# The expert products of a metaformer block in full fp32 on 64-row tiles, with paired transposes and no split of the second normalization

## The reference

```python
x = x + attention(_ln_c(x))            # over the 16 images at each position, 8 heads of 16 channels, gated
t = x as tokens                        # 65536 rows of 64
t = t + L0_ffn(_ln_t(t))               # 8 experts, the best 2 of each token
x = x + L1_conv(_ln_c(x))              # expand 64 -> 128, running mean along an axis, sigmoid gate, 64 -> 64
t = t + L1_ffn(_ln_t(t))               # 32 experts that each pick 8 tokens of an image
```

```python
def _L0_ffn_ref(x, router_w, router_b, expert_w, expert_b):
    router_probs = jax.nn.softmax(x @ router_w + router_b, axis=-1)
    top_p, top_i = jax.lax.top_k(router_probs, K)                  # K = 2 of 8
    top_p = top_p / jnp.sum(top_p, axis=-1, keepdims=True)
    expert_out = jnp.einsum('bnd,edc->bnec', x, expert_w) + expert_b
    gathered = jnp.take_along_axis(expert_out, top_i[..., None], axis=2)
    return jnp.einsum('bnk,bnkc->bnc', top_p, gathered)
```

## Time and profile before

| what | value |
|---|---|
| three runs | 3127.79, 3136.28 and 3141.26 us |
| median | 3136.28 us |
| span of the profiled execution | 3121.5 us |
| busy PE (matmul) | 2647.5 us, 85% |
| busy PE (weight load) | 1969.9 us, 63% |
| busy DVE | 2551.6 us, 82% |
| busy POOL | 2161.0 us, 69% |
| busy ACT | 2005.1 us, 64% |

### The profile page before, as it was taken

The page is one execution under the profiler, slowest core; times in us unless marked ns, Lnnn a source line. Parts: engine busy times, 40 slices in busy tenths (PEclk is TensorE's granted clock), DMA queues, the critical chain, the costliest instruction groups (busy, mean ns, idle before and its releaser), DMA issues. The chain is left out here.

```text
span 3121.5 us, 108500 instructions
## 1 busy us (share of the span) xinstructions
PE 2647.5 (85%) x37071; PEld 1969.9 (63%) x37071; DVE 2551.6 (82%) x9002; ACT 2005.1 (64%) x3590; POOL 2161.0 (69%) x2963
## 2 busy tenths in 40 slices
PE   2898898888888888898898898888988988896697
PEld 2666666666666656666666666666666666664586
DVE  2788889888888898888888888888889888885604
ACT  2666767766676676776776766677667676762600
POOL 2677777877777777777787877778777777863000
PEclk9788988887888888888887987889889788885858
DMA  0011101111011010110101111011010010101828
GB/s 17 9 20 18 19 17 19 19 18 19 17 19 18 18 19 17 19 19 18 19 17 18 19 18 19 17 19 19 18 19 18 17 19 18 19 15 19 269 96 337
DMA packets 263153, 106.67 MB, mean 34 GB/s; under 512 B 250257, under 2 KB 254900, under 8 KB 258997
## 3 DMA queue, kind: packets, MB, share of 16 engines
q1 hardware_dynamic: 260933, 93.16, 12.9%
q10 hardware_dynamic: 2160, 12.68, 1.0%
HBM read 55.31 MB, written 50.33 MB: 34 GB/s over the span
## 5 line engine op out<-in xcount | busy, mean ns | idle before, releaser
L472 ACT ACTIVATE kT<-s_bank,b_k,block_of 128x512 f32<-128x512 f32 x1024 | 748.8, 771 | 3.6 <-PE s_bank L609 0.3
L640 PE MATMUL s_bank<-kT,qT 128*32 128x128 f32 x8192 | 396.1, 372 | 187.3 <-issue 187.3
L640 PEld LDWEIGHTS s_bank<-kT,qT 128*32 128x32 f32 x8192 | 349.5, 152 | 226.8 <-issue 224.7
L489 ACT ACTIVATE qT<-shared,b_qkg 128x256 f32<-128x256 f32 x256 | 107.5, 471 | 412.0 <-PE shared L609 412.0
L811 DVE TENSOR_REDUCE mixed<-yg 128x256 f32<-128x2048 f32 x128 | 288.5, 2254 | 0.2
L687 PEld LDWEIGHTS o_bank<-w_o,ogT 128*128 128x128 f32 x2048 | 247.9, 193 | 23.7 <-DVE ogT L839 14.8
L414 POOL TENSOR_TENSOR probs<-weights,own_den 128x1024 f32<-128x1024 f32 x128 | 252.7, 1975 | 1.8 <-DVE own_den L857 1.8
L687 PE MATMUL o_bank<-w_o,ogT 128*128 128x64 f32 x2048 | 246.9, 274 | 4.3 <-DVE ogT L839 3.9
L387 POOL TENSOR_TENSOR split_ffn<-norm_ffn,split_ffn 128x256 fp32r<-128x256 f32 x128 | 93.6, 731 | 215.1 <-ACT split_ffn L464 215.1
L658 PEld LDWEIGHTS o_bank<-probsT,v_sb 32*32 32x32 f32 x16384 | 170.2, 107 | 63.7 <-issue 58.1
L658 PE MATMUL o_bank<-probsT,v_sb 32*32 32x64 f32 x16384 | 196.5, 234 | 1.5 <-DVE yg L932 1.5
(11 more groups left out here) (204 smaller groups left out, 7648.6 us busy)
## 6 DMA issues: line engine op xcount, KB each, us to landing
x_in<-in_x SPq DMA_DIRECT2D x1024, 16.0 KB, 1.7
x_scratch<-x SPq DMA_DIRECT2D x1024, 16.0 KB, 1.4
normalized_x_scratch<-norm_pick SPq DMA_DIRECT2D x1024, 16.0 KB, 1.5
xa<-normalized_x_scratch SPq DMA_DIRECT2D x16, 1024.0 KB, 8.1
xb<-x_scratch ACTq DMA_DIRECT2D x8, 1024.0 KB, 10.3
out_x<-xa SPq DMA_DIRECT2D x16, 512.0 KB, 5.3
out_x<-xb SPq DMA_DIRECT2D x16, 512.0 KB, 6.9
xa<-x_scratch SPq DMA_DIRECT2D x4, 1024.0 KB, 6.5
```

Source lines behind the costliest of these rows:

```text
L472: ins = s.activation(kT[:, h, :], bk("k")[:], ACT.Identity, bias=b_k[:, h:h + 1], scale=block_of[:, h:h + 1])
L640: ins = t_.matmul(s_bank[g * 32:(g + 1) * 32, 0, t * P:(t + 1) * P], qT[z][:, c, tok:tok + 32], kT[:, :, tok + c * N:tok + (c + 1) * N], s ...
```

## The change

The expert layer's second operand is no longer split. Four things follow from that.

- **Transposes.** `paired` transposes two token tiles of 64 channels at once: the result has the channels of an even tile on rows 0 to 63 and those of the odd tile after it on rows 64 to 127. Two transposes take the place of four, they wait for the normalization itself, and `tT` is half as wide and in plain fp32.
- **Experts.** A tile is one fp32 product on 64 rows (0 to 63 for y0 and y2, 64 to 127 for y1 and y3) in the place of two one-pass products on 128 rows. As an fp32 product it counts once in the order of instructions below. Weights, the bias rows (`bias3`) and the ones stand in both halves; in the program as built the bias product is on the same 64 rows.
- **Router.** `w_router2` is a block matrix, with the router's weights once for the rows 0 to 63 and once for 64 to 127, so that one product gives the logits of two tiles.
- **Split and order.** The rounding copy of ACT and the subtraction of POOL for `ffn` go. In TURNS, `expand` and `y0` change places, and so in PE's list.

Setup gains a second load of `bias3`, two fills and two small copies, and loses a subtraction and a rounding copy. The diff, cut to its core:

```diff
-TURNS = ["att_t", "q", "ffn_t", "v", "scan_out", "gate", "pick", "conv_t", "y0", "expand", "y3"]
+TURNS = ["att_t", "q", "ffn_t", "v", "scan_out", "gate", "pick", "conv_t", "expand", "y0", "y3"]
...
-            w_expert_hi, w_expert_lo = cb("w_expert_hi", [P, NE * D], F32R), cb("w_expert_lo", [P, NE * D], F32R)
+            w_expert_ce = cb("w_expert_ce", [P, NE * D])
+            w_router2 = cb("w_router2", [P, 2, NE])
...
-            bias3 = cb("bias3", [3, NE * D], BF16)
+            bias3 = cb("bias3", [P, NE * D], BF16)
-            ones3 = cb("ones3", [3, P], BF16)
+            ones3 = cb("ones3", [P, P], BF16)
...
-            KINDS = ("att", "ffn", "conv", "pick")
+            KINDS, SPLIT = ("att", "ffn", "conv", "pick"), ("att", "conv")
-            split = {k: cpair(f"split_{k}", [P, QT, 2, D], F32R) for k in KINDS[:3]}
+            split = {k: cpair(f"split_{k}", [P, QT, 2, D], F32R) for k in SPLIT}
...
-            tT = cpair("tT", [P, QTOK], F32R)
+            tT = cpair("tT", [P, QTOK // 2])
...
-                sp.dma_start(bias3[:], bias_parts[:]).then_inc(s_bias3, 16)
+                for k in range(2):
+                    sp.dma_start(bias3[k * D:k * D + 3], bias_parts[:]).then_inc(s_bias3, 16)
...
                 def step(i, q):
                     if runs(i, q, 4):
                         normalize("ffn", x1[par(q, 4)], 1.0, 1e-5, i, q, 4, "ffn_t")
-                    if runs(i, q, 4):
-                        second_part("ffn", i, q, 4)
...
-                    if runs(i, q, 4):
-                        round_part("ffn", i, q, 4, "ffn_t")
...
                         wait(act, filled["y3"], at(i, q, 6))
-                        s.copy(tT[z][:], bk("ffn_t")[:]).then_inc(drained["ffn_t"], 1)
+                        s.copy(tT[z][:], bk("ffn_t")[:, 0:QTOK // 2]).then_inc(drained["ffn_t"], 1)
...
+                def paired(name, kind, i, q, lag):
+                    for u in range(2):
+                        ins = t_.transpose(bank_of(q, name)[:, u * P:(u + 1) * P],
+                                           norm[kind][par(q, lag)][:, 2 * u:2 * u + 2, :].rearrange("p t d -> p (t d)"), ident[:])
+                    ins.then_inc(filled[name], 1)
...
                             bank_free(pe, i, q, y)
-                        t_.matmul(bk(y)[:], ones3[:], bias3[:], start=True, stop=False)
-                        t_.matmul(bk(y)[:], tT[z4][:, tile(t)], w_expert_hi[:], start=False, stop=False)
-                        t_.matmul(bk(y)[:], tT[z4][:, tile(t)], w_expert_lo[:], start=False, stop=True).then_inc(filled[y], 1)
+                        r0 = t % 2 * D
+                        t_.matmul(bk(y)[:], ones3[r0:r0 + D], bias3[r0:r0 + D], start=True, stop=False)
+                        t_.matmul(bk(y)[:], tT[z4][r0:r0 + D, tile(t // 2)], w_expert_ce[r0:r0 + D], start=False,
+                                  stop=True).then_inc(filled[y], 1)
...
                     if runs(i, q, 4):
                         bank_free(pe, i, q, "ffn_t")
-                        pe.wait_ge(s_split["ffn"], at(i, q, 4))
-                        transposed("ffn_t", "ffn", i, q, 4)
+                        pe.wait_ge(s_norm["ffn"], at(i, q, 4))
+                        paired("ffn_t", "ffn", i, q, 4)
                         bank_free(pe, i, q, "v")
...
                         pe.wait_ge(drained["ffn_t"], at(i, q, 4))
-                        for t in range(QT):
-                            ins = t_.matmul(bk("route")[:, t * NE:(t + 1) * NE], tT[z4][:, tile(t)].bitcast(F32), w_router[:])
+                        for u in range(2):
+                            ins = t_.matmul(bk("route")[:, 2 * u * NE:2 * (u + 1) * NE], tT[z4][:, tile(u)],
+                                            w_router2[:].rearrange("p h e -> p (h e)"))
                         ins.then_inc(filled["route"], 1)
...
                         bank_free(pe, i, q, "conv_t")
                         transposed("conv_t", "conv", i, q, 5)
-                    if runs(i, q, 4):
-                        experts(0)
                     if runs(i, q, 5):
                         bank_free(pe, i, q, "expand")
...
                         t_.matmul(bk("expand")[:], w_expand_hi[:], cT[:], start=True, stop=False)
                         t_.matmul(bk("expand")[:], w_expand_lo[:], cT[:], start=False, stop=True).then_inc(filled["expand"], 1)
                     if runs(i, q, 4):
-                        for t in range(1, QT):
+                        for t in range(QT):
                             experts(t)
...
-                v.tensor_copy(w_expert_hi[:].rearrange("d (c e) -> d c e", e=NE), w_expert[:].rearrange("d e c -> d c e"))
+                setup(v.tensor_copy(w_expert_ce[:].rearrange("d (c e) -> d c e", e=NE), w_expert[:].rearrange("d e c -> d c e")))
+                v.memset(w_router2[:], 0.0)
+                v.memset(bias3[:], 0.0)
-                setup(v.tensor_tensor(by_channel(w_expert_lo[:]), w_expert[:].rearrange("d e c -> d c e"),
-                                      by_channel(w_expert_hi[:].bitcast(F32)), ALU.subtract))
+                for h in range(2):
+                    rows = slice(h * D, (h + 1) * D)
+                    setup(v.tensor_copy(w_router2[rows, h, :], w_router[rows]))
```

More of the change, by code:

```diff
@@ L177, in build @@
             s_norm = {k: sem(f"normalized_{k}") for k in KINDS}
-            s_hi = {k: sem(f"rounded_{k}") for k in KINDS[:3]}
-            s_split = {k: sem(f"split_{k}") for k in KINDS[:3]}
+            s_hi = {k: sem(f"rounded_{k}") for k in SPLIT}
+            s_split = {k: sem(f"split_{k}") for k in SPLIT}
             s_scores, s_sub, s_exp, s_rden, s_probs, s_probsT = (sem("scores_filled"), sem("scores_read"), sem("exp_done"),
@@ L191, in build @@
             N_POOL_SETUP = 12
-            N_DVE_SETUP = 11
+            N_DVE_SETUP = 13
             def at(i, q, lag, n=1, more=0):
@@ L588, in _ @@
                 pe.wait_ge(s_dve_setup, N_DVE_SETUP)
-                pe.wait_ge(s_bias3, 16)
+                pe.wait_ge(s_bias3, 32)
                 def transposed(name, kind, i, q, lag):
```

## The result

The changed kernel takes 3176.30 us (median of 3174.70 to 3180.22) against 3136.28: ratio 1.0127, 95% interval 1.0093 to 1.0162. It is slower by 1.3%, where no change to speak of was forecast. The profiled execution has a span of 3174.6 us against 3121.5. PE is busy 2547.2 us and POOL 2041.4, 100 and 120 less than before, DVE 2550.6 as before: the work went, and the time grew by waits.

A forecast was written before the change was run, and what follows sets the result against it. It took a turn's period as a PE part plus an ACT part. Terms -14, -18, -3, +25 and +1 sum to -9 on 3136.28: 3127 us, own range 3100 to 3150, all cases 3050 to 3190.

The forecast's parts named there:

- the order: Expand ahead of y0: y1 full earlier -14 us, gpre no longer waiting for expand -3, y3 behind ACT's drain +25.
- the rest of the change: Two transposes fewer in PE's part, -18 us, and setup +1; work off ACT and POOL and the router's products counted nothing.
- The y3 term: y3 waits for ACT to drain expand; scores 1.2 us late in 21 of 64 odd turns, +25 us, bounds 0 to 77.
- own sign of being wrong: The prediction called itself wrong if, among other signs, y3 proved slow in most odd turns.
- The second rival: y3 behind ACT's drain becomes the bound in every odd turn: +77 instead of +25, 3179 us; chance 0.20.
- The term on the order: Expert stretch of 25 even turns where ema_t waits for the scan: y1 full 0.56 us earlier, -14 us.
- the first rival: The clock stays up, since products side by side keep PE busier where it fell: 3051 us; chance 0.20.
- the 18 us of the sum: Second normalization's transposes, four to two: 0.22 us off in 63 turns and 0.11 in 40, -18 us.

The follow-up runs named there:

- x2: Changed kernel with the old order, y0 before expand in both the bank list and PE's program; 3011.93 us, ratio 0.9606.
- x1: Changed kernel with y0 before expand again in the bank list only, PE's program order kept; 3164.95 us, ratio 1.0084.
- x6: Changed kernel with four unused bias products added between conv_t and expand, where PE stands idle; 3064.12 us, ratio 0.9722.
- x13: x2 with its two ffn_t transposes and two router products issued twice; 3065.49 us, ratio 0.9770.
- x7: x2 with one wait more: y0 also waits for ACT's copy cT; 3180.94 us, ratio 1.0101.
- x12: Kernel before with each tile's two one-pass products made one fp32 product on the same 128 rows; 3098.76 us, ratio 0.9876.
- x8: x2 with seven unused bias products added ahead of the scores in odd turns; 3183.35 us, ratio 1.0109.
- x10: Kernel before with two unused bias products added ahead of y0; 3136.70 us, ratio 0.9992.
- x3: Kernel before with the order alone changed, expand ahead of y0 in the bank list and PE's program; 3187.10 us, ratio 1.0166.

## Why the prediction was wrong

**Two errors against each other.** The sum has the order at +8 (-14, -3 and +25) and the rest of the change at -17. Measured by x2, the order costs 164 us and the rest gives 124. Both parts were off by over 100 us in opposite directions; that the sum came within 49 us is luck.

**The y3 term was mis-sized.** It had y3 at the lower clock in 21 of 64 odd turns, +25. In all 57 odd turns measured PE stands idle ahead of y3, att_t behind it runs at the lower clock (1.11), and the scores of the next turn start 1.04 to 1.26 us after the last key copy, 1.17 in the mean, where it was 0.20 before: 64 x 0.97 = 62, and x1 takes 63 off the odd turns. The prediction's own sign of being wrong, y3 slow in most odd turns, came true. The second rival has this mechanism and 3179, with a measured 3176, but the agreement is luck too: x1 takes the wait away and its median is 11 us lower, not 77.

**The term on the order failed.** It had y1 full 0.56 earlier in the 25 slow even turns, -14. In the low turn shown y1 is full 17.53 after the turn's start (1123.22), against 17.92 in the earlier trace rows, 0.39 earlier; over the even turns of the two profiles it is 0.19 later (16.50 against 16.31). And y0, side by side with it, is full no earlier, and DVE's read of y0, 0.6 us, moved behind y1. The text followed y1 and not y0's reader.

**The hole ahead of expand was given no term.** This is the step that cost most. The prediction named idle time before expand only as an argument against a clock that stays up. y0 had covered the wait for cT; without it PE stands 0.94 us in each turn, in the place of 0.43 ahead of y0, and 28 even turns are low in the place of 19. x6 prices the hole: filled, the changed kernel is 112 us faster, and no even turn is low. Without the hole the changed kernel would have been near the first rival, 3051.

**What held.** Two transposes take 0.28 (1068.03 - 1067.75) in place of 0.49; their worth, with the router's products, is larger than the 18 us of the sum (x13: 53). The tiles run side by side: y2's bias starts 1.09 behind y0's (1076.73 to 1077.82), where 1.2 was forecast. ACT, with less to do, waits longer for PE (467.1 us before qT against 412.0). Even turns hang on y1: over the kernels of the table their length goes with the time at which y1 is full (correlation 0.94), within a kernel with a correlation of 0.95 to 1.00 over its 57 even turns, x7 apart, in which they are all alike.

## What to carry to other kernels

Before moving work on an in-order engine, ask what the moved piece was covering: in x2, where y0 fills the wait for cT, no even turn is low; with that wait left open, in the changed kernel, 28 of 57 are. Look for the turn that is sensitive, and see that the low stretch of the clock falls in the other; a mean clock does not show it (over its span 0.913 in x12 and 0.883 in x2, which is 87 us faster; 0.858 to 0.859 in the four runs of x1, which take 3137 to 3179 us). Two tiles side by side are full at the same time (here within 0.01 us), so their reader can start later on the first.

The best version found is the change with the old order (x2), 3012 us, 4% under the kernel before.

## What was not expected of the hardware

Products on the two row halves start 0.01 us apart and alternate pass by pass: y1's bias starts at 1120.91 and its first pass at 1121.32, before y0's second pass at 1122.16. The Trainium skill, "TensorE: Matmul & The Clock Gate", Part 3, has matmuls start and end strictly in the order of the queue; here y1's bias, which stands behind y0's passes in the program, starts before them, so the trace does not agree. The Trainium skill, "TensorEngine Tiling (Array Packing)", Key Properties, says that different tiles can load and multiply in parallel, and by the same rows the trace agrees.

Work added made the kernel faster (x6 by 3.5%), and work added to hold the clock elsewhere made it slower (x8 by 5.7% over x2). Why the clock falls in the expert stretch of the kernel before even with the small hole filled (x10), and why the same hole lowers fewer even turns in x3, stays open.
